# Attention mask and mixture of experts on one core: filler products between batch 0's transposed masks and its first expert slot left out

## The reference

```python
# layer 1: learned sparse adjacency
Q = (h @ Wq.T), K = (h @ Wk.T)                    # h = context, 4 heads of 16
sim = einsum('bhnd,bhmd->bnm', Q, K) / (sqrt(16) * 4)
threshold = top_k(sim, 76)[0][:, :, -1:]
A = sigmoid(sim) * (sim >= threshold)
A = (A + swapaxes(A, -1, -2)) * 0.5
x = x + (1 - g) * layernorm(x) + g * A            # g = sigmoid(gamma)
# layer 2: mixture of experts on z = layernorm(x)
scores = softmax(z @ gate_w.T); weights, idx = top_k(scores, 2)
y = sum over 8 experts of comb[e] * (silu(z @ w1[e].T) * (z @ w3[e].T)) @ w2[e].T
s = (silu(z @ ws1.T) * (z @ ws3.T)) @ ws2.T       # one shared expert
x = x + y + s
```

## Time and profile before

| | us |
|---|---|
| median of 3 runs | 116.22 (116.21 to 116.55) |
| the profiled execution | 115.1 |
| its span, first to last instruction | 113.3 |
| PE busy | 104.7 (92% of the span) |
| VectorE busy | 85.7 (76%) |
| GpSimd busy | 70.4 (62%) |
| ScalarE busy | 62.5 (55%) |
| mean granted TensorE clock | 0.97 |

### The profile page before, as it was taken

The page is one execution under the profiler, slowest core; times in us unless marked ns, Lnnn a source line. Parts: engine busy times, 40 slices in busy tenths (PEclk is TensorE's granted clock), DMA queues, the critical chain, the costliest instruction groups (busy, mean ns, idle before and its releaser), DMA issues.

```text
span 113.3 us, 2526 instructions
## 1 busy us (share of the span) xinstructions
PE 104.7 (92%) x824; PEld 102.2 (90%) x824; DVE 85.7 (76%) x278; ACT 62.5 (55%) x157; POOL 70.4 (62%) x141
## 2 busy tenths in 40 slices
PE   6999618989999998999999999999999999999990
PEld 6799608978999998999999999999999999999990
DVE  6689779799998799967829999739536989456631
ACT  4179999989769864459793218233512452035400
POOL 4047688795964996599898494596109442283700
PEclk9999975599999999999999999999999999999999
DMA  1699993000002800000009100010281103830002
GB/s 35 157 343 365 363 362 108 3 6 3 0 0 72 292 14 0 3 0 6 0 4 301 68 3 6 26 66 0 64 299 50 64 3 95 270 103 0 0 0 93
DMA packets 8158, 10.33 MB, mean 91 GB/s; under 512 B 1936, under 2 KB 6544, under 8 KB 8144
## 3 DMA queue, kind: packets, MB, share of 16 engines
q1 hardware_dynamic: 7776, 10.13, 27.7%
q10 hardware_dynamic: 368, 0.04, 0.3%
HBM read 9.09 MB, written 1.08 MB: 90 GB/s over the span
## 4 chain that ended last, share of the span: by engine, by line
PE 75%; ACT 12%; DVE 8%; issue 2%; POOL 0%; POOLq 0%
PE ps_h L1378 22%; PE ps_u L1378 21%; PE ps_y L1406 20%; PE ps_a L1406 3%; PE ps_c L1345 3%; PE ps_u L1269 2%; ACT qkT L578 2%; ACT up_hi L556 1%; ACT sig L605 1%; PE ps_a L1316 1%; PE ps_b L1328 1%; DVE near L968 1%; DVE chosen L1085 1%; PE ps_h L1278 1%; ACT sides L627 1%
## 5 line engine op out<-in xcount | busy, mean ns | idle before, releaser
L453 POOL TENSOR_TENSOR gc<-prod,weights 128x512 f32<-128x512 f32 x16 | 25.8, 1630 | 16.4 <-DMA weights<-gates 9.2
L703 ACT ACTIVATE sil<-ps_h 128x512 f32<-128x512 f32 (+1 forms) x20 | 10.9, 552 | 16.7 <-PE ps_h L1378 16.7
L714 ACT ACTIVATE g_hi<-gc 128x512 fp32r<-128x512 f32 x16 | 10.0, 627 | 16.4 <-POOL gc L453 16.4
L1406 PE MATMUL ps_y<-dn_hi,g_hi 128*128 128x256 f32 x63 | 17.8, 283 | 0.0
L1406 PE MATMUL ps_y<-dn_hi,g_lo 128*128 128x256 f32 x63 | 17.7, 281 | 0.0
L1406 PE MATMUL ps_y<-dn_lo,g_hi 128*128 128x256 f32 x63 | 17.7, 280 | 0.0
L1130 DVE TENSOR_TENSOR g_lo<-gc,g_hi 128x512 fp32r<-128x512 f32 x16 | 13.9, 866 | 3.1 <-ACT g_hi L714 2.5
L1378 PE MATMUL ps_h<-z_hi,up_hi 128*128 128x256 f32 x72 | 15.3, 294 | 0.4 <-DVE prod L1118 0.4
L1378 PE MATMUL ps_h<-z_lo,up_hi 128*128 128x256 f32 x72 | 14.5, 282 | 0.2 <-DVE z_lo L1061 0.2
L1378 PE MATMUL ps_u<-z_hi,up_hi 128*128 128x256 f32 x72 | 14.4, 281 | 0.0
L1378 PE MATMUL ps_u<-z_hi,up_lo 128*128 128x256 f32 x72 | 14.4, 281 | 0.0
(11 more groups left out here) (199 smaller groups left out, 252.8 us busy)
## 6 DMA issues: line engine op xcount, KB each, us to landing
weights<-gates SPq DMA_DIRECT2D x8, 512.0 KB, 4.8
x_sb<-in_x SPq DMA_DIRECT2D x4, 256.0 KB, 6.3
up_raw<-in_w1t SPq DMA_DIRECT2D x4, 256.0 KB, 5.7
up_raw<-in_w3t SPq DMA_DIRECT2D x4, 256.0 KB, 5.9
dn_raw<-in_w2t SPq DMA_DIRECT2D x4, 256.0 KB, 6.3
out_x<-fin SPq DMA_DIRECT2D x3, 256.0 KB, 2.1
out_x<-fin SPq DMA_DIRECT2D x2, 128.0 KB, 1.7
ctx_sb<-in_ctxT SPq DMA_DIRECT2D x1, 192.0 KB, 4.7
```

The lines of the kernel that those rows point to most:

```text
L453: nc.gpsimd.tensor_tensor(gc[k % 2][:, :].rearrange("p (n t q) -> p n t q", n=2, t=T), prod[s][:, :].rearrange("p (n t q) -> p n t q", n=2 ...
L703: nc.scalar.activation(sil[i % 2][:, :w], ps_h[i % 2][:, :w], ACT.Silu).then_inc(silu_ready, 1)
L714: nc.scalar.activation(g_hi[s][:, :], src[:, :], ACT.Copy).then_inc(ghi0_ready if s == 0 else ghi_ready, 1)
L1406: last = nc.tensor.matmul(dst[:, t * D:(t + 1) * D], g[s][:, tok], w[:, e, :], start=(s == 0 and first and m == 0), stop=(s == SLOTS - 1 a ...
```

## The change

Four calls of keep_warm are left out of PE's order: one product after batch 0's transposed masks, seven after similar(3), one after sum_hits(1) and four after transpose_z(0), 13 products in all. The eight other calls stay, the one after logits(0) among them.

```diff
@@ -1438,13 +1438,9 @@
             sum_hits(0)
             keep_warm(2)
             transpose_masked(0)
-            keep_warm(1)
             similar(3)
-            keep_warm(7)
             sum_hits(1)
-            keep_warm(1)
             transpose_z(0)
-            keep_warm(4)
             up(0, 0)
             logits(0)
             keep_warm(1)
```

## The result

| | before | changed |
|---|---|---|
| median, us | 116.22 (115.45 to 116.55, 4 runs) | 120.88 (120.14 to 121.69, 4 runs) |
| the profiled execution | 115.1 | 120.14 |
| its span | 113.3 | 118.3 |
| mean granted TensorE clock | 0.97 | 0.913 |
| TensorE busy | 104.7 | 106.0 |

The changed kernel is slower by a factor of 1.0437 (95% interval 1.0384 to 1.0489). The median lost 4.66 us, the profiled execution 5.04 us. The forecast was 117.8 with a range to 119.0: the sign was right, the size wrong by a factor of three.

The account below looks back on a forecast made before the run. TensorE was taken to bound the kernel from 26.46 us. Direct gain 0 plus a half-clock shift of 3.06 - 1.49 = 1.57 us on the median 116.22 gave 117.8 us, range 116.8 to 119.0 (8 in 10).

Parts of the forecast that it names:

- What bounds the kernel, and that the loss is kept: TensorE carries the path from 26.46 us; no later wait absorbs its loss, so the whole +1.6 us stays.
- Nothing to gain from the removal: The 13 fillers cost nothing on the path; only 0.31 us touches a dependency, and the direct gain is 0.
- Steps 1 and 2: Hit products and transposes from 23.50 us at half clock, then z_hi: up(0, 0) starts at 26.12 instead of 25.53.
- Step 3: Expert-slot products at half clock: 233 ns each against 118, by the similarity's ratio of 1.97.
- Step 4: Dense part from 26.12 us: shift is R - [26.46 - 0.47 + (R - 26.12)/1.97], giving 1.57 us.
- R: Moment full clock returns in the dense part: 27.1 to 31.0 us, taken as 29.05.
- my lower bound of 3.6 us: Earliest clock rise after work starts, read from the kernel's start, where the rise lay between 4.55 and 6.34 us.
- The rival "returns later": up(0, 0)'s start or light products don't count as work; a rise at 33 costs 3.5 us, 119.7; chance 0.12.
- The wait near 44.6: TensorE's wait for prod on VectorE, 0.37 us before 42.99 in the kernel before, moves along and stays about 0.4 us.
- The rival of no effect: Left-out fillers cover nothing; hit products and transposes restore full clock by 26.1 us: 116.2 to 116.6; chance 0.07.
- the faster one: VectorE's comparison at 40.92 takes 0.18 us, not 1.21, closing TensorE's 0.37 us wait: 115.85; chance 0.03.

Follow-up runs that it names:

- the two singles: Kernel before without only the single fillers behind transpose_masked(0) and behind sum_hits(1): 115.68 us against 115.62, ratio 0.9984.
- two fillers: Changed kernel with two fillers put between transpose_z(0) and up(0, 0): 116.56 us median against 115.77 of before, ratio 1.0058 leaving out three slow executions.
- the narrow fillers: Kernel before with the 13 fillers of the four calls cut from 128 to 16 columns: 121.21 us median.
- prod first: gate_values(0, 3) ahead of route_a(1) in VectorE's order: in the changed kernel 120.35 us median of six; in the kernel before 115.03 us, ratio 0.9924.
- the seven alone: Changed kernel with only the seven fillers behind similar(3) put back: 119.29 us median, 1.0267 of before.

## Why the prediction was wrong

- **What bounds the kernel, and that the loss is kept.** Right. PE from 26 us on carries the end; 4.50 us at 44.04 became 5.03 at the end, nothing was absorbed.
- **Nothing to gain from the removal.** Right. In the changed kernel up(0, 0) came no earlier, and without the two singles the time is 0.9984 of before (0.9951 to 1.0017), where the 0.31 us ahead of transpose_z(0) would be 0.0027.
- **Steps 1 and 2, entry at half clock.** Right to 0.03 us: hit products at 23.53, transposes at 24.37, up(0, 0) at 26.15 for 26.12 (the terms of step 2 add up to 26.14). The clock did not rise at 22.3, and PE rested 3.37 us where I had 3.6. That it would not rise without the seven fillers was in part luck. In the profile with two fillers the same work raised it at 21.0, though only until 24.4.
- **Step 3, the rate.** 0.213 us per product, not 0.233: a ratio of 1.81, where I took 1.97 from the similarity's rows. The other form's row was a poor stand-in. The Trainium skill's "TensorE: Matmul & The Clock Gate", "Back-to-back issue gap", gave the 213 ns that this trace now shows.
- **Step 4 and the return.** Here it failed, at the term R, the moment at which the clock returns. I took the two rises of the trace, 3.6 and 4.9 us after work began, as the measure, let the count begin with the hit products or with up(0, 0), and put the return at 27.1 to 31.0. It came at 35.66, 9.5 us after up(0, 0) began. With R = 35.66 and the rate of 1.81, the formula gives 9.67 - 9.51/1.81 = 4.42, and 4.50 was measured: the formula was good, its R was not. What I left out of R is that the kind of work can matter and that the moment isn't fixed. With the narrow fillers the engine was as busy and no return came before 37.0. From the start of up(0, 0) it took 9.5 us in the changed kernel, 9.4 in the profile of it with prod first, and 7.6 in that with two fillers. With up(0, 1) drawn ahead it took 3.2. With the rest before 17.3 us filled it took 3.4, and there the logits stood in their old place. And my lower bound of 3.6 us from the start of work was none: with two fillers it took 2.7. Why the changed kernel's return is as late as 9.5 us is open. The work between its two wide stretches may be a part of it; no run shows that by itself.
- **The rival "returns later".** It named light products as the cause, which the narrow fillers bear out for fillers and no run for the logits, and a return at 33 with 3.5 us. I gave it 0.12, since "no rise in the trace took over 4.9 us". That was two rises, and no evidence about how late one can come. The range, to 119.0, cut it off.
- **The wait near 44.6 "still about 0.4".** Wrong by 0.43: it stood at 47.92 and took 0.80. I had assumed that VectorE's slow small operation moves with PE. How long it takes goes with where GpSimd's products stand, and these did not move by the same amount: from 40.45 to 43.22, 2.77 us, where VectorE's lgx moved by 4.51.
- **The rival of no effect** and **the faster one** are out. Of the latter the place was right: with prod first the wait of 0.37 us is gone, and without the filler behind logits(0) the comparison takes the 0.18 us of its twin, as that rival had it.

So the profiled loss of 5.04 us is 4.50 from the half clock, 0.43 from this wait and 0.11 in what follows. The median's 4.66 I can't split in the same way: the changed kernel's executions had 17 or 20.5 us cold, and those of 17 were no faster (120.83 and 121.69 against 120.14 and 120.92). The profile with prod first shows one way in which that can be: the 3.4 us are missing at the covered end. How the moment of the return is drawn in each execution is open; no run here steers it.

## What to carry to other kernels

Count filler work by its place, not by its sum. Here 7 products raised the clock and 4 held it up to the first dense work; the 2 in other places did nothing that could be measured, and leaving out one where the engine is never idle gave some 0.3%, not clear of noise. When such cover is taken away, don't price the return of the clock by one or two rises of a single trace. Here it came 3.4 and 9.5 us after the first dense products began, in two versions that have the same work from there on. Take the late end into the range, and look at several executions, since one profile shows one course of the clock. And a sum of half clock over an execution is no price: half clock costs only where the engine is what the end waits for.

## What the runs showed of the hardware

- The rest ahead of a fall has no fixed length here. The clock went down 1.0 us after the last product in the kernel before, 0.7 us after it in the changed one, and 3.9 us after it where 13 fillers had closed the rest before 17.3 us (19.3 to 23.2). It also went down while PE was busy, at 27.8 with the seven alone and at 20.1 in the profile of the changed kernel with prod first.
- With 14 narrow MATMULs busy for 3.01 us at 20.93, and no rest over 0.2 us from there to the dense work, the clock stayed at 1.2 GHz until 37.0.
- The records print full clock for the kernel's first microseconds, and the projection's 1.19 us at 3.36 against 0.60 at 6.34 contradicts them; the changed kernel repeats it.
- A float32 transpose does run at either level: four start to start in 0.43 us at 2.4 GHz and 0.88 at 1.2.
- A VectorE copy of four columns took 1.62 us beside a GpSimd product of the same length, and 0.16 at 40.31 of the kernel before, ahead of that product.
